# Quantised FFN: GpSimd adds the output bias to the rows only when VectorE has rounded the first group for the second half

## What is computed

```python
x_sim = quantize_a16(x)                  # one scale from the largest |x| of all
hidden = gelu(x_sim @ W_in_sim + b_in, approximate=False)
hidden_sim = quantize_a16(hidden)        # one scale from the largest |hidden| of all
out = hidden_sim @ W_out_sim + b_out
x = x + tanh(g_ffn[0]) * out             # x inside the FFN was layer-normalised
```

## Time and profile before

| what | value |
|---|---|
| time, median of 3 runs (lowest to highest) | 1506.33 us (1505.86 to 1507.77) |
| time of the profiled execution | 1505.87 us |
| its span, first to last instruction | 1504.1 us |
| busy over the span: PE, DVE, ACT, POOL | 1448.8, 1081.3, 897.5, 635.3 us |
| this FFN's first half in the trace | about 624 to 683 us |
| its second half in the trace | 684.7 to 748.8 us |
| the 16 bias additions on GpSimd | 668.2 to 688.6 us |

### The profile page before, as it was taken

One profiled execution on the slowest core, in us unless ns is written; L12 is line 12 of the kernel. 1 busy time (PEld: TensorE's weight loads), 2 busy tenths in 40 slices (PEclk: granted clock), 3 DMA queues, 4 the chain that ended last, 5 costly groups with the idle time before them and its releaser, 6 DMA issues. The chain is left out here.

```text
span 1504.1 us, 27527 instructions
## 1 busy us (share of the span) xinstructions
PE 1448.8 (96%) x9390; PEld 1215.2 (81%) x9408; DVE 1081.3 (72%) x2327; ACT 897.5 (60%) x1904; POOL 635.3 (42%) x758
## 2 busy tenths in 40 slices
PE   9999999999999999879999999999999999999997
PEld 8888788888888877638978888888888888778886
DVE  4677876676767668899866666676766666776886
ACT  4666666666666654591056666666666666556662
POOL 1333334443334344573023434333333343455885
PEclk9999999999999999999999999999999999999999
DMA  7665544444444432300065444445444444320011
GB/s 224 191 181 161 158 136 144 143 142 149 131 156 126 156 118 86 89 0 2 3 189 167 132 157 130 157 131 161 131 155 132 154 130 151 103 70 8 28 35 43
DMA packets 202787, 182.72 MB, mean 121 GB/s; under 512 B 12368, under 2 KB 201808, under 8 KB 202640
## 3 DMA queue, kind: packets, MB, share of 16 engines
q1 hardware_dynamic: 202080, 180.91, 38.3%
q10 hardware_dynamic: 576, 0.13, 0.0%
HBM read 95.74 MB, written 85.25 MB: 120 GB/s over the span
## 5 line engine op out<-in xcount | busy, mean ns | idle before, releaser
L1122 POOL TENSOR_TENSOR PN<-E,RC 128x512 f32<-128x512 f32 x378 | 331.2, 904 | 494.7 <-DVE RC L1080 494.7
L1029 DVE TENSOR_REDUCE MX<-pS 128x6 f32<-128x462 f32 (+1 forms) x384 | 222.2, 579 | 275.9 <-PE pS L649 275.9
L764 ACT ACTIVATE G<-pP 128x308 f32<-128x308 f32 (+1 forms) x488 | 208.6, 428 | 243.7 <-PE pP L518 243.4
L687 PE MATMUL pO<-work,PT 128*128 128x128 f32 (+1 forms) x2560 | 329.2, 276 | 15.9 <-ACT PT L847 15.9
L687 PEld LDWEIGHTS pO<-work,PT 128*128 128x128 f32 (+1 forms) x2560 | 307.5, 191 | 22.9 <-issue 20.5
L649 PE MATMUL pS<-G,XT 128*128 128x462 f32 (+1 forms) x768 | 324.4, 507 | 0.0
L838 ACT ACTIVATE E<-E 128x462 f32<-128x462 f32 (+1 forms) x384 | 209.5, 546 | 112.7 <-DVE E L1039 104.5
L516 PE MATMUL pP<-Chi,Ahi 128*128 128x308 f32 x496 | 239.2, 482 | 1.4 <-ACT G L764 1.2
L1039 DVE TENSOR_TENSOR E<-pS,MX 128x462 f32<-128x462 f32 (+1 forms) x384 | 223.4, 582 | 8.9
L847 ACT ACTIVATE PT<-pT 128x512 f32<-128x512 f32 (+1 forms) x384 | 200.2, 522 | 40.4 <-PE pT L672 40.3
L1077 DVE TENSOR_REDUCE SM<-E 128x16 f32<-128x1232 f32 (+1 forms) x144 | 184.8, 1290 | 43.6 <-ACT E L838 42.5
(11 more groups left out here) (230 smaller groups left out, 2018.5 us busy)
## 6 DMA issues: line engine op xcount, KB each, us to landing
values<-ST SPq DMA_DIRECT2D x256, 256.0 KB
work<-values SPq DMA_DIRECT2D x512, 128.0 KB
values<-ST SPq DMA_DIRECT2D x64, 208.0 KB
work<-values SPq DMA_DIRECT2D x128, 104.0 KB
C<-in_ctx SPq DMA_DIRECT2D x32, 154.0 KB
X<-in_x SPq DMA_DIRECT2D x16, 256.0 KB, 5.2
out<-s_O SPq DMA_DIRECT2D x16, 256.0 KB, 2.3
work<-in_L_xattn_Wq SPq DMA_DIRECT2D x2, 512.0 KB, 6.2
```

The source lines that it names most:

```text
L687: last = nc.tensor.matmul(pO[:, 0:CH], PT[0:rows, c, :], V[(t - 1) % VRING][0:rows, tile, CH * hh:CH * hh + CH], start=c == 0, stop=c == C ...
L764: return nc.scalar.activation(G[0:live, g % 2, :, head, :], bank[0:live, 0:KEYCOLS].rearrange("p (b k) -> p b k", k=KEYS), ACT.Copy)
L1029: nc.vector.tensor_reduce(MX[:, h0:h1], pS[u][:, 0:(h1 - h0) * KEYS].rearrange("p (h k) -> p h k", k=KEYS), X_AXIS, ALU.max).then_inc(max_ ...
L1122: nc.gpsimd.tensor_tensor(out, e, scale, ALU.mult).then_inc(prob_ready, 1)
```

## The change

GpSimd waits, before the first of the 16 additions, until `hq_ready` has reached GROUP, that is 4: the four pieces of group 0 have been rounded by VectorE. Nothing else is changed, and no instruction of the computation is added or taken away.

```diff
             for g in range(GROUPS):
                 normalise(g)
             pool.wait_ge(gbias_made, 1)
+            pool.wait_ge(hq_ready, GROUP)
             for g in range(GROUPS):
                 rows = p["X"][:, g * GROUP:(g + 1) * GROUP, :]
                 nc.gpsimd.tensor_tensor(rows, rows, gbias[:, :].unsqueeze(1).to_broadcast([128, GROUP, CH]),
```

## The result

The changed kernel takes 1508.47 us (median of 20 runs, 1507.48 to 1510.03), the one before 1506.21 us (20 runs, 1505.58 to 1508.0): ratio 1.0015, 95% interval 1.0009 to 1.0022. So it is slower, by 2.3 us, which is less than the 0.2% that I had set as the bound of "the same". The forecast was +3.6 us; the range, 1506.8 to 1512.6 us, held the time.

The account below looks back on a forecast made before the run. VectorE was taken to bound the first half, TensorE the second. Group 1 starting on TensorE 3.34 us earlier, then 25.2 us becoming 32.2 up to group 8, gave +3.6 us, 1509.9 us; range 1506.8 to 1512.6 us.

Parts of the forecast that it names:

- Gain in front of the second half: End of first half: two slow quantise instructions fall back to 0.48 us, 1.23 us less on VectorE.
- Turns at the wide roundings: Second half, groups 3 to 8: VectorE and GpSimd alternate, 4.42 us a group with two additions, against TensorE's 3.61.
- The rival in which VectorE keeps its turn from L1420 to L1423: Second half: no addition gets between a group's two roundings, 3.47 us a group; -3.2 us, 1503.1 us; chance 0.09.
- the one in which the wide roundings lose less than the narrow ones: Second half: 2048-wide roundings lose about half of the 0.8 us a group; about +0.5 us, 1506.8 us; chance 0.15.
- The other size of the prediction: Second half, by a Trainium skill page: 1.39 us in place of 1.13 per addition, 4.94 us a group, 1512.7 us.
- The clock: TensorE idling before groups 1 and 2 lowers its clock: +1 us more, 1510.9 us; a rival, chance 0.13.
- the first turn: At 687.0 us GpSimd goes ahead of group 1's first rounding: +4.4 us, 1510.7 us; a rival, chance 0.08.
- Group 2: L1420 starts 1.23 us behind the end of L1423: Start of group 2's rounding: addition 3 gets in just before VectorE asks, so the group is rounded at 696.06 us.
- one of my rivals, at a chance of 0.12: Group 2: addition 3 comes too late, 4.42 us in place of 5.66; +2.4 us, 1508.7 us; chance 0.12.

Follow-up runs that it names:

- e1: Changed kernel without the 16 bias additions and the residual's wait for them: 1501.75 us, ratio 0.9972.
- e5: Changed kernel with all 16 additions released once the first half's last quantise is done, instead of after group 0's rounding: 1508.75 us, ratio 1.0017.
- e7: Changed kernel with additions 0 to 7 released after the last quantise, 8 to 15 together when group 0 is rounded: 1505.49 us, ratio 0.9994.
- e6: Changed kernel with 22 identity products in place of 12 behind the second spread, making TensorE 2.24 us later with group 0: 1509.92 us, ratio 1.0024.

## Why the prediction was right, and where it was not

- *Gain in front of the second half*: as worked out. 1.24 us in the first half, L1421 of group 1 at 686.66 (686.65 forecast, less the 0.26 us of shift), group 0 on TensorE without a break at full clock.
- *Turns at the wide roundings*: as worked out from the narrow ones. 1.13 and 1.08 us, 4.42 us a group with two additions, TensorE the bound again from group 8. e1, e5 and e7 show it from three sides. The rival in which VectorE keeps its turn from L1420 to L1423 falls: L1424 takes 2.17 us. So does the one in which the wide roundings lose less than the narrow ones: both lose 0.94 us. The other size of the prediction, 4.94 us a group and 1512.7 us, didn't come either: it put a delay behind the rounding on top of the addition's full 1.27 us, and only 1.13 us pass in all.
- *The clock*: it didn't fall at the gaps of 1.55 us in front of group 1 and 0.6 us later on. GpSimd didn't have the first turn either.
- *The step that failed* is "Group 2: L1420 starts 1.23 us behind the end of L1423". It came 0.83 us behind it (690.97 against 690.14), 0.3 us ahead of the end of addition 2, and addition 3 was too late. So group 2 was rounded 4.42 us after group 1, not 5.66, and the sum is 3.6 - 1.24 = +2.4 us, against 2.45 in the trace and 2.3 in the medians. That was one of my rivals, at a chance of 0.12, but I had worked out its margin from the same wrong row. The range was wide enough for either course of addition 3, so that the time fell inside it says nothing for this step.
- *Why that row misled*: I took the 1.23 us from the earlier trace rows as VectorE's own, with the tiny product in it. It held a wait of 0.44 us, which the kernel before's timeline of VectorE puts down to that product:

```profile
693.43 0.21 DVE L1434 TENSOR_SCALAR small<-sh,gate_f 128x1 f32<-128x1 f32 x1
694.07 0.75 DVE L1430 SCALAR_TENSOR_TENSOR X<-u_pu,small,X 128x512 f32<-128x512 f32 x1 [0.44 <-DVE small L1434]
```

  In fact residual 0 waited for TensorE, whose group 0 was late by its waits and the low clock: 24 records from 689.40 for 4.57 us end at 693.97, and the residual started at 694.07. The change itself took that lateness away. e1 shows the gap gone with TensorE on time, and e6 brings it back by delaying TensorE alone: 0.71 us, again put down to the tiny product, and the 1.24 us with it.

The sign was right. The size stayed within 0.2% of no change, a result to which I had given a chance of 0.34; to slower by more than that I had given 0.58.

## What to carry to other kernels

Where GpSimd and VectorE exclude each other, count instructions of VectorE that meet GpSimd, not the time that both are busy: each pays for a whole GpSimd instruction or the rest of one, so put GpSimd's work beside reductions and PSUM reads, and cut it so that one piece fits in the gap. A wait that takes such work out of a stage bound by VectorE only helps if the stage that receives it has room; here there were 0.39 us a group, and free running took 0.8 more than that. When a duration is taken over into another schedule, first ask whether it holds a wait that the change removes; the engine named for a wait of several semaphores need not be the one that was late.

## What was not expected of the hardware

- An instruction seems not to ask for its turn at the moment at which its record starts. In e5 L1413's record starts at 683.70, 0.12 us ahead of the end of an addition at 683.82, and yet the next addition went first: L1413 ended at 685.32, 0.28 behind the end of that one (683.76 + 1.28 = 685.04). A record that started 0.3 us ahead of the end did get the turn (changed kernel, 690.97 against 691.27). Where between these two the moment lies was not measured.
- An addition of 128x256 takes 0.72 us against 1.27 for 128x512, so some 0.17 us of each is fixed, if the rest goes with the width (an estimate from these two durations).
